# Attention loop: GpSimd forms the low weights of even slots, one maximum a slot, key projections every second slot

## The chip, the cores and the metric

The kernel runs on one core of one Trainium2 chip. The metric is the device time of one execution in microseconds (us). The engines are TensorE (PE, with its weight loads as PEld), VectorE (DVE), ScalarE (ACT), GpSimd (POOL) and SyncE (SP), which issues the transfers (DMA). Each runs its own instructions in order and waits on semaphores.

## The reference, cut to what matters

One layer in three parts, each added to x: a cross attention of 256 rows on 4096 context rows with 16 heads, a causal self attention, and routed experts. The change is in the first.

```python
kv_rope = kv_c * cos[None] + _rotate_half(kv_c) * sin[None]
q_r = jnp.einsum('bshq,hqr->bhsr', q_big, W_qr)
k_r = jnp.einsum('bld,hdr->bhlr', kv_rope, W_kr)
scores = jnp.einsum('bhsr,bhlr->bhsl', q_r, k_r)
attn = jax.nn.softmax(scores, axis=-1)
ctx_c = jnp.einsum('bhsl,bld->bhsd', attn, kv_rope)
```

## The kernel before, in words

Matmuls run in bf16, with each fp32 operand held as a high part and a low part (value minus high part). The heads are taken in 8 pairs. A pair is 16 slots; slots 0 to 7 are its first head, 8 to 15 its second, and a slot covers 512 context rows by 256 query rows.

For each slot, `scores` (PE, L944 and L945) writes one of two PSUM buffers `psS`; ACT takes the exponential twice, once as bf16 (`p_hi`, L491) and once as fp32 (`p_f`, L493); DVE forms `p_lo` = `p_f` minus `p_hi` (L687); `context_hi` (PE, L957 and L958) and `context_lo` (L965) add weights times values into the PSUM tile `psC`, a view of `psO[0]`. PE computes the scores of slot s + 1 at the start of slot s. After 8 slots the head's sums are copied out of `psC` (`head_out`, ACT, L484), a reciprocal is formed (DVE, L680) and GpSimd scales (`normalise`, L411). `context_hi` of the next head waits for that copy.

Beside this, the loop prepares the next pair. Its rotated keys come in 8 chunks of 512 rows: `keys` (PE, L903 to L905) writes the one bank `psO[1]`; ACT writes the high part `k_hi` (`keys_high`, L472); DVE writes the low part `k_lo` and so frees the bank (`keys_low`, L663, semaphore `s_kfree`). The softmax needs a bound on each row. For this, 16 `maximum` steps (two a chunk) each run two matmuls into `psM` (PE, L917) and one maximum over it (DVE, L669); `psM` is held once, so the next step's matmuls wait for the DVE. At the end DVE negates the maxima (L672, L674), PE turns them into a row (`bias`, L925), and ACT copies that row into row 64 of `q2` (`bias_rows`, L477), which the next pair's first `scores` waits for.

`keys` and `maximum` write shared `k_hi` and `k_lo`; the scores read copies of them. SP makes the copies in `copy_keys(q)` with DMAs from on-chip memory to on-chip memory: for each head j of the pair and each half of the chunks three transfers (L327 to L329), and for each head two more for its queries (L330, L331). SP issues them in this order and waits before each group of three:

```python
wait_apart(sp, s_kfree, q * CHUNKS + CHUNKS // 2 * (half + 1), sp_passed)
wait_apart(sp, s_scores, (q - 1) * SLOTS + HALF * j + HALF // 2 * (half + 1), sp_passed)
```

`keys_high` overwrites `k_hi`, so for the first chunk of a half it waits until both heads' copies of that half for the pair before are done:

```python
if c % (CHUNKS // 2) == 0:
    wait(act, k_copied[0][c // (CHUNKS // 2)], q * 48)
    wait(act, k_copied[1][c // (CHUNKS // 2)], q * 48)
```

The order of the work is written out by hand in the four `body` functions, one an engine. Before the change: chunk c is projected in slot c of the pair before, its `keys_high` and `keys_low` come one slot later, maxima 0 to 7 stand in slots 2 to 9 and two a slot in slots 10 to 13, the bias in slot 14. Pair 0 is written out, pairs 1 to 6 are a hardware loop, and pair 7, which prepares nothing, is written out.

Of the kernel before, what the change touches and what calls it, by code (L numbers as in the profile page):

```python
# [10 lines left out]
BF16 = mybir.dt.bfloat16  # L11
ACT = mybir.ActivationFunctionType
ALU = mybir.AluOpType
# [51 lines left out]
def maxima_in(slot):  # L65

    if 2 <= slot < 10:
        return [slot - 2]
    return [2 * slot - 12, 2 * slot - 11] if 10 <= slot < 14 else []


BIAS_SLOT = 14
# [50 lines left out]
def layer(nc, a, out):  # L123
    with ExitStack() as ctx:
# [13 lines left out]
        def cut(cols, at=None):  # L138
# [68 lines left out]
        raw = arena[:, top[0]:top[0] + TT * CW].rearrange("p (s w) -> p s w", s=TT)  # L207
        wo2 = cut(DC * D).rearrange("p (c n) -> p c n", c=DC)
# [52 lines left out]
        s_scores, s_phi, s_pf, s_plo, s_pv, s_out = (  # L261
            sem(n) for n in ("s_scores", "s_phi", "s_pf", "s_plo", "s_pv", "s_out"))
# [4 lines left out]
        qmax_copied = sem("qmax_copied")  # L267
# [110 lines left out]
        def _(pool):  # L378
# [12 lines left out]
            def bring(q):  # L391

                wait_apart(pool, s_mmm, q * MAXIMA, pool_passed)
                h = q * 2
                nc.gpsimd.tensor_copy(q_max, q1_all[:, bass.ds(h, 2), :]).then_inc(qmax_copied, 1)
                nc.gpsimd.tensor_copy(wkr_now[:, 0, :], wkr_hi[:, bass.ds(q * P, P)]).then_inc(qmax_copied, 1)
                nc.gpsimd.tensor_copy(wkr_now[:, 1, :], wkr_lo[:, bass.ds(q * P, P)]).then_inc(qmax_copied, 1)
            pool.wait_ge(qhi_done, 2)
# [15 lines left out]
            normalise(0)  # L414
            with pool.Fori(2, NPAIR) as q:
                bring(q)
                normalise(q * 2 - 3)
                normalise(q * 2 - 2)
            for h in range(H - 3, H):
                normalise(h)  # L420
# [11 lines left out]
        def _(act):  # L432
# [41 lines left out]
            def bias_rows(q):  # L474

                act.wait_ge(s_tmm, q + 1)
                nc.scalar.copy(q2[R:R + 1, :, :], psM[R:R + 1, :].rearrange("p (j s) -> p j s", j=2)[:, :, 0:T]).then_inc(s_bias, 1)  # L477

            def head_out(p, j):

                hd = p * 2 + j
                act.wait_ge(s_pv, hd * HALF + HALF)
                wait(act, ctx_done, hd)
                nc.scalar.copy(raw, psC).then_inc(s_out, 1)  # L484

            def body(p, ahead=True):
                for s in range(SLOTS):
                    t = p * SLOTS + s
                    act.wait_ge(s_scores, t + 1)
                    wait(act, s_pv, t - 1)  # L490
                    nc.scalar.activation(p_hi[:, s % 2, :], psS[s % 2][:, :], ACT.Exp).then_inc(s_phi, 1)  # L491
                    wait(act, s_plo, t - 1)
                    nc.scalar.activation(p_f[:, s % 2, :], psS[s % 2][:, :], ACT.Exp).then_inc(s_pf, 1)  # L493
                    if s == HALF:
                        head_out(p, 0)
                    if s == 0 and not (isinstance(p, int) and p == 0):
                        head_out(p - 1, 1)
                    if ahead and 1 <= s <= CHUNKS:
                        keys_high(p + 1, s - 1)
                    if ahead and s == BIAS_SLOT + 1:  # L500
                        bias_rows(p + 1)
            for what, n, *rest in BEFORE:
                if what == "rope":
                    rope_high(n)
                elif what == "k":
                    keys_high(0, n)
                elif what == "t":
                    bias_rows(0)
                elif what != "m" and (what != "hk" or rest[0] == DC - 1):
                    query(what, n)  # L510
            body(0)
            with act.Fori(1, NPAIR - 1) as p:
                body(p)
            body(NPAIR - 1, ahead=False)
            head_out(NPAIR - 1, 1)

# [78 lines left out]
        def _(dve):  # L595
# [80 lines left out]
            def one_over_sum(p, j):  # L676
                hd = p * 2 + j
                dve.wait_ge(s_out, hd + 1)
                wait(dve, ctx_done, hd)
                nc.vector.reciprocal(rsum, raw[:, :, K]).then_inc(s_rsum, 1)  # L680

            def body(p, ahead=True):
                for s in range(SLOTS):
                    t = p * SLOTS + s
                    dve.wait_ge(s_pf, t + 1)
                    wait(dve, s_pv, t - 1)
                    nc.vector.tensor_tensor(p_lo[:, s % 2, :], p_f[:, s % 2, :], p_hi[:, s % 2, :], ALU.subtract).then_inc(s_plo, 1)  # L687
                    if s == HALF:
                        one_over_sum(p, 0)
                    if s == 0 and not (isinstance(p, int) and p == 0):  # L690
                        one_over_sum(p - 1, 1)
                    if ahead and 1 <= s <= CHUNKS:
                        keys_low(p + 1, s - 1)
                    if ahead:
                        for m in maxima_in(s):
                            maximum(p + 1, m)
# [13 lines left out]
            body(0)  # L710
            with dve.Fori(1, NPAIR - 1) as p:
                body(p)
            body(NPAIR - 1, ahead=False)
            one_over_sum(NPAIR - 1, 1)
# [136 lines left out]
        def _(pe):  # L851
# [43 lines left out]
            def keys(q, c):  # L895

                first = isinstance(q, int) and q == 0
                bank = psE[c % 2] if first else psO[1]
                wait(pe, s_kfree, q * CHUNKS + c - (1 if first else 0))
                if c == 0:  # L900
                    pe.wait_ge(qmax_copied, q * 3 + 3)
                n = slice(512 * c, 512 * c + 512)
                mm(bank[:, :], wkr_now[:, 0, :], kt_hi[:, n], start=True, stop=False)  # L903
                mm(bank[:, :], wkr_now[:, 0, :], kt_lo[:, n], start=False, stop=False)
                mm(bank[:, :], wkr_now[:, 1, :], kt_hi[:, n], start=False, stop=True).then_inc(s_kmm, 1)  # L905

            def maximum(q, m):

                c, st = m // TT, m % TT
                wait(pe, s_mfree, q * MAXIMA + m)  # L910
                if m == 0:
                    wait(pe, s_bias, q)
                if st == 0:
                    pe.wait_ge(s_khi, q * CHUNKS + c + 1)
                for j in range(2):
                    r = slice(R * j, R * j + R)
                    last = mm(psM[:, 512 * j:512 * j + 512], q_max[r, j, P * st:P * st + P], k_hi[r, 512 * c:512 * c + 512], start=True, stop=True)  # L917
                last.then_inc(s_mmm, 1)

            def bias(q):  # L920

                pe.wait_ge(s_negm, q + 1)
                for j in range(2):
                    for st in range(TT):
                        last = mm(psM[R:R + 1, 512 * j + P * st:512 * j + P * st + P], negm[:, TT * j + st:TT * j + st + 1], ident_b, start=True, stop=True)  # L925
                last.then_inc(s_tmm, 1)
# [21 lines left out]
            def context_hi(p, s):  # L948
# [5 lines left out]
                for i in range(GROUP):  # L954
                    for st in range(TT):
                        ph = p_hi[:, s % 2, T * i + P * st:T * i + P * st + P]
                        mm(psC[:, st, :], ph, vx[:, GROUP * g + i, 0:CW], start=g == 0 and i == 0 and st == 0, stop=False, skip_group_check=True)  # L957
                        mm(psC[:, st, 0:K], ph, vx[:, GROUP * g + i, CW:VW], start=False, stop=False, skip_group_check=True)  # L958

            def context_lo(p, s):  # L960
                g, t = s % HALF, p * SLOTS + s
                pe.wait_ge(s_plo, t + 1)
# [6 lines left out]
            def body(p, ahead=True):  # L969
                for s in range(SLOTS):  # L970
                    now = maxima_in(s) if ahead else []
                    if s < SLOTS - 1:
                        scores(p, s + 1)
                    if now:
                        maximum(p + 1, now[0])
                    context_hi(p, s)
                    if s == SLOTS - 1 and ahead:
                        scores(p, SLOTS)
                    if ahead and s < CHUNKS:
                        keys(p + 1, s)  # L980
                    context_lo(p, s)
                    if now[1:]:
                        maximum(p + 1, now[1])
                    if ahead and s == BIAS_SLOT:
                        bias(p + 1)
            for what, n, *rest in BEFORE:
# [11 lines left out]
                elif what == "t":  # L998
                    bias(0)
                else:  # L1000
                    query(what, n, *rest)
# [3 lines left out]
            body(0)  # L1005
            with pe.Fori(1, NPAIR - 1) as p:
                body(p)
            body(NPAIR - 1, ahead=False)
# [286 lines left out]
```

## Time and profile before

| | us |
|---|---|
| median of three runs | 741.29 (740.64 to 742.59) |
| profiled execution | 741.01, its span 739.2 |
| PE, DVE, ACT, POOL busy | 654.4, 453.2, 384.5, 49.7 |
| mean granted TensorE clock | 0.979 of full speed; 1.00 in every stretch from 0 to 500 us |

The span runs from the first to the last instruction. Busy time counts overlaps once. The exponentials of the attention loop begin at 85.5 us and its last head is scaled at 502.2 us; the self attention and the experts follow.

### The profile page before, as it was taken

How to read it: one execution, taken by the hardware profiler on the slowest of the kernel's cores; microseconds unless marked ns; L12 is line 12 of the kernel's file. 1: busy time of each engine (PE TensorE's matmuls, PEld its weight loads, DVE VectorE, ACT ScalarE, POOL GpSimd, SP SyncE). 2: the span in 40 equal slices, each digit the busy share in tenths (PEclk: the TensorE clock that was granted, in tenths of full speed). 3: DMA queues.
4: the chain of work that ended last, by engine and by line, in shares of the span. 5: the costliest groups of instructions: out<-in, count | busy, mean ns of one | idle time of the engine just before them, and what ended most of it. 6: DMA issues, size and time to landing. Idle time of an engine off the chain costs nothing.

```text
span 739.2 us, 14931 instructions
## 1 busy us (share of the span) xinstructions
PE 654.4 (89%) x5890; PEld 461.1 (62%) x5890; DVE 453.2 (61%) x594; ACT 384.5 (52%) x567; POOL 49.7 (7%) x71
## 2 busy tenths in 40 slices
PE   5799899899898898898998998998978988899766
PEld 4666576676776776776776776885546856442211
DVE  2977598688688688698688687452127836211001
ACT  2543676676675675775775774882117842200000
POOL 2430000000000000000000000000002210000000
PEclk9999999999999999999999999999989989999989
DMA  8902794224224224233143143008980031299991
GB/s 360 418 26 43 172 336 99 49 45 91 49 43 90 48 46 87 48 64 79 38 82 79 24 93 80 7 2 327 416 348 4 1 115 57 104 395 419 415 418 68
DMA packets 25250, 105.04 MB, mean 142 GB/s; under 512 B 3712, under 2 KB 6912, under 8 KB 19200
## 3 DMA queue, kind: packets, MB, share of 16 engines
q1 hardware_dynamic: 25216, 104.57, 43.8%
q8 instruction: 24, 0.39, 0.2%
q14 instruction: 10, 0.08, 0.0%
HBM read 77.29 MB, written 0.52 MB: 105 GB/s over the span
## 4 chain that ended last, share of the span: by engine, by line
PE 59%; DVE 18%; issue 8%; ACT 7%; DMA 3%; SPq 3%; POOL 1%; DVEq 0%; ACTq 0%
PE psO L957 7%; PE psO L965 6%; DVE arena L669 6%; PE psO L958 5%; PE psS L945 5%; PE psS L944 5%; PE psM L917 5%; DVE arena L687 5%; PE psO L1029 4%; DMA arena<-w_exp 3%; SPq L351 3%; PE psS L1171 3%; PE psO L881 2%; PE psO L903 2%; PE psO L905 2%
## 5 line engine op out<-in xcount | busy, mean ns | idle before, releaser
L687 DVE TENSOR_TENSOR arena<-arena 128x1024 bf16<-128x1024 f32 x128 | 156.7, 1224 | 79.8 <-ACT arena L493 78.1
L491 ACT ACTIVATE arena<-psS 128x1024 bf16<-128x1024 f32 x128 | 131.2, 1025 | 113.2 <-PE psS L945 112.9
L669 DVE TENSOR_REDUCE arena<-psM 128x2 f32<-128x1024 f32 x128 | 155.9, 1218 | 14.8 <-PE psM L917 14.8
L957 PE MATMUL psO<-arena 128*128 128x129 bf16 x1024 | 133.4, 220 | 7.6 <-ACT arena L484 7.2
L958 PE MATMUL psO<-arena 128*128 128x128 bf16 x1024 | 132.5, 220 | 0.0
L493 ACT ACTIVATE arena<-psS 128x1024 f32<-128x1024 f32 x128 | 130.6, 1021 | 0.0
L944 PE MATMUL psS<-arena 128*128 128x256 bf16 x512 | 120.8, 273 | 0.8 <-ACT arena L477 0.8
L945 PE MATMUL psS<-arena 65*128 65x256 bf16 x512 | 120.8, 273 | 0.0
L957 PEld LDWEIGHTS psO<-arena 128*128 128x128 bf16 x1024 | 98.0, 98 | 30.3 <-issue 20.7
L958 PEld LDWEIGHTS psO<-arena 128*128 128x128 bf16 x1024 | 99.4, 97 | 0.4
L965 PE MATMUL psO<-arena 128*128 128x129 bf16 x1024 | 79.4, 220 | 8.8 <-DVE arena L687 8.4
L965 PEld LDWEIGHTS psO<-arena 128*128 128x128 bf16 x1024 | 65.2, 97 | 25.0 <-DVE arena L687 11.8
L917 PE MATMUL psM<-arena 64*128 64x512 bf16 x256 | 49.9, 386 | 16.2 <-DVE arena L669 15.8
L944 PEld LDWEIGHTS psS<-arena 128*128 128x128 bf16 x512 | 50.2, 98 | 12.4 <-issue 4.8
L945 PEld LDWEIGHTS psS<-arena 65*128 65x128 bf16 x512 | 50.1, 98 | 5.4
L917 PEld LDWEIGHTS psM<-arena 64*128 64x128 bf16 x256 | 12.3, 92 | 45.8 <-DVE arena L669 25.2
L1171 PE MATMUL psS<-arena 128*32 128x512 f32 x256 | 32.3, 649 | 8.4 <-DMA arena<-w_exp 7.9
L663 DVE TENSOR_TENSOR arena<-psO,arena 128x512 bf16<-128x512 f32 x56 | 38.2, 683 | 0.6
L567 ACT ACTIVATE arena<-psS 128x256 f32<-128x256 f32 x8 | 3.1, 383 | 64.2 <-PE psS L1171 64.2
L881 PE MATMUL psO<-arena 128*128 128x256 f32 x128 | 34.5, 400 | 0.7 <-ACT arena L440 0.7
L838 DVE TENSOR_TENSOR arena<-psS,arena 128x256 f32<-128x256 f32 x8 | 3.4, 424 | 51.4 <-ACT arena L567 51.4
L472 ACT CAST arena<-psO 128x512 bf16<-128x512 f32 x56 | 32.9, 588 | 3.1
(191 smaller groups left out, 767.9 us busy)
## 6 DMA issues: line engine op xcount, KB each, us to landing
arena<-w_exp SPq DMA_DIRECT2D x32, 1024.0 KB, 15.3
arena<-arena SPq DMA_DIRECT2D x96, 256.0 KB, 3.7
arena<-w_exp SPq DMA_DIRECT2D x32, 512.0 KB, 17.5
arena<-w_pair SPq DMA_DIRECT2D x8, 1088.0 KB, 16.8
arena<-w_o SPq DMA_DIRECT2D x1, 4096.0 KB, 21.1
arena<-w_shared SPq DMA_DIRECT2D x3, 1024.0 KB, 5.3
arena<-ctx SPq DMA_DIRECT2D x4, 512.0 KB, 13.5
arena<-rope SPq DMA_DIRECT2D x4, 512.0 KB, 14.3
```

The lines of the kernel that those rows point to most:

```text
L491: nc.scalar.activation(p_hi[:, s % 2, :], psS[s % 2][:, :], ACT.Exp).then_inc(s_phi, 1)
L493: nc.scalar.activation(p_f[:, s % 2, :], psS[s % 2][:, :], ACT.Exp).then_inc(s_pf, 1)
L669: nc.vector.reduce_max(maxes[:, :, st, c], psM[:, :].rearrange("p (j n) -> p j n", j=2), AX.X).then_inc(s_mfree, 1)
L687: nc.vector.tensor_tensor(p_lo[:, s % 2, :], p_f[:, s % 2, :], p_hi[:, s % 2, :], ALU.subtract).then_inc(s_plo, 1)
L881: last = mm(psO[h % 2][:, 0:T], wq[:, c, K * j:K * j + K], xnT[:, c, :], start=c == 0, stop=c == DC - 1)
L917: last = mm(psM[:, 512 * j:512 * j + 512], q_max[r, j, P * st:P * st + P], k_hi[r, 512 * c:512 * c + 512], start=True, stop=True)
L944: mm(o, k1[:, j, l], q1[:, j, :], start=True, stop=False)
L945: last = mm(o, k2[0:R + 1, j, l], q2[0:R + 1, j, :], start=False, stop=True)
L957: mm(psC[:, st, :], ph, vx[:, GROUP * g + i, 0:CW], start=g == 0 and i == 0 and st == 0, stop=False, skip_group_check=True)
L958: mm(psC[:, st, 0:K], ph, vx[:, GROUP * g + i, CW:VW], start=False, stop=False, skip_group_check=True)
L965: last = mm(psC[:, st, :], p_lo[:, s % 2, T * i + P * st:T * i + P * st + P], vx[:, GROUP * g + i, 0:CW], start=False, stop=g == HALF - 1 ...
L1171: last = mm(psF[g % 2][SLOT * j:SLOT * j + SLOT, :], xpT[:, c, CAP * e:CAP * e + SLOT], ring[e % RING][:, 2 * FI * c:2 * FI * (c + 1)], st ...
```

## The change

A table made by `plan` now says for each slot which chunks and which maxima of the next pair (1) and of the pair after that (2) stand in it. In the steady loop chunk c of the next pair stands in slot 2c - 4 for c from 2 to 7, maximum m from 2 to 15 in slot m - 2, and the first two chunks of the pair after next in slots 12 and 13, its first two maxima in slots 14 and 15. `keys_high` and `keys_low` now stand in the slot of their `keys`. GpSimd forms `p_lo` of the even slots, DVE that of the odd ones. `context_lo` of an even slot comes at the end of the next slot, that of an odd slot in the next slot behind `scores`. DVE takes `head_out` and `bias_rows` over from ACT, and the bias row is written to `psO[1]`. The exponential into `p_hi` waits for `context_hi` (`s_hi`) instead of `context_lo`. GpSimd brings a second set of queries and key weights for the early chunks. `copy_keys` and the waits in `keys_high` stay. Pairs 1 to 5 are the loop; pairs 0, 6 and 7 are written out.

```diff
+def plan(first, after):
+    keys = [(1, c, c if first else 2 * c - 4) for c in range(0 if first else 2, CHUNKS)]
+    keys += [(2, c, SLOTS - 4 + c) for c in range(2)] if after else []
+    at = [2, 3, 4, 4, 5, 6, 6, 7, 8, 8, 9, 10, 10, 11, 12, 13] if first else [None, None, *range(BIAS_SLOT)]
+    maxima = [(1, m, slot) for m, slot in enumerate(at) if slot is not None]
+    maxima += [(2, m, BIAS_SLOT + m) for m in range(2)] if after else []
+ENTRY, STEADY, LAST_BUT_ONE, LAST = plan(True, True), plan(False, True), plan(False, False), [[[], []]] * SLOTS
...
+            def low_part(p, s):
+                wait_apart(pool, s_pf, p * SLOTS + s + 1, pool_passed)
+                wait_apart(pool, s_pv, p * SLOTS + s - 1, pool_passed)
+                nc.gpsimd.tensor_tensor(p_lo[:, s % 2, :], p_f[:, s % 2, :], p_hi[:, s % 2, :], ALU.subtract).then_inc(s_plo[0], 1)
+            def body(p, after=True):
+                for s in range(0, SLOTS, 2):
+                    if s == 0 and not (isinstance(p, int) and p == 0):
+                        normalise(p * 2 - 1)
+                    if s == HALF:
+                        normalise(p * 2)
+                    low_part(p, s)
+                    if after and s == 4:
+                        bring_next(p + 2)
+                    if after and s == BIAS_SLOT - 2:
+                        bring(p + 2)
...
 (ACT, in body)
-                    wait(act, s_pv, t - 1)
+                    wait(act, s_hi, t - 1)
+                    wait(act, s_plo[s % 2], p * HALF + s // 2)
-                    wait(act, s_plo, t - 1)
-                    if ahead and 1 <= s <= CHUNKS:
-                        keys_high(p + 1, s - 1)
+                    for d, c in todo[s][0]:
+                        keys_high(p + d, c)
...
 (DVE, in body; head_out comes first in slots 0 and 8)
+                    if s == BIAS_SLOT and todo is not LAST:
+                        bias_rows(p + 1)
+                    for d, m in maxima[0:1]:
+                        maximum(p + d, m)
+                    if s % 2:
+                        dve.wait_ge(s_pf, t + 1)
+                        wait(dve, s_pv, t - 1)
+                        nc.vector.tensor_tensor(p_lo[:, s % 2, :], p_f[:, s % 2, :], p_hi[:, s % 2, :], ALU.subtract).then_inc(s_plo[1], 1)
+                    for d, c in keys:
+                        keys_low(p + d, c)
+                    for d, m in maxima[1:2]:
+                        maximum(p + d, m)
...
 (PE, in body)
+                    key_steps, maxima = todo[s]
                     if s < SLOTS - 1:
                         scores(p, s + 1)
+                    elif todo is not LAST:
+                        scores(p, SLOTS)
+                    if s % 2 == 0 and s:
+                        context_lo(p, s - 1)
+                    if s == 0 and not (isinstance(p, int) and p == 0):
+                        context_lo(p - 1, SLOTS - 1)
+                    if s == BIAS_SLOT and todo is not LAST:
+                        bias(p + 1, todo is not LAST_BUT_ONE)
+                    for d, m in maxima[0:1]:
+                        maximum(p + d, m)
+                    for d, c in key_steps:
+                        keys(p + d, c)
                     context_hi(p, s)
+                    for d, m in maxima[1:2]:
+                        maximum(p + d, m)
+                    if s % 2:
+                        context_lo(p, s - 1)
```

The order of ACT in the loop, slots 7 to 10 before: L491 and L493 are the exponentials, L484 is `head_out`, L472 is `keys_high`, whose first waits of the pair stand in slot 1.

```order
L491 ACTIVATE arena<-psS 128x1024 [waits s_pv,s_scores]
L493 ACTIVATE arena<-psS 128x1024 [waits s_plo]
L482 ISA
L484 COPY arena<-psO 128x258 [waits ctx_done,s_pv]
L467 REGISTER_ALU
L472 CAST arena<-psO 128x512 [waits s_kmm]
L489 REGISTER_ALU
L491 ACTIVATE arena<-psS 128x1024 [waits s_pv,s_scores]
L493 ACTIVATE arena<-psS 128x1024 [waits s_plo]
L489 REGISTER_ALU
L491 ACTIVATE arena<-psS 128x1024 [waits s_pv,s_scores]
```

Slots 12 and 13 of ACT after the change, where the first two chunks of the pair after next stand (L511 and L512 are the exponentials, L503 is `keys_high`):

```order
L511 ACTIVATE arena<-psS 128x1024 [waits s_plo_even]
L512 ACTIVATE arena<-psS 128x1024
L498 ISA
L114 REGISTER_ALU [waits s_kmm]
L503 CAST arena<-psO 128x512 [waits k_copied10,k_copied00]
L508 REGISTER_ALU
L511 ACTIVATE arena<-psS 128x1024 [waits s_plo_odd,s_hi,s_scores]
L512 ACTIVATE arena<-psS 128x1024
L498 REGISTER_ALU
L503 CAST arena<-psO 128x512 [waits s_kmm]
```

The copy out of `psC` is gone from ACT, and the first chunk's `keys_high`, with its wait for the copies of both heads, stands in front of the exponentials of slot 13.

The order of DVE in the loop, slots 9 to 11 before: L687 is `p_lo`, L669 the maximum.

```order
L687 TENSOR_TENSOR arena<-arena 128x1024 [waits s_pv,s_pf]
L668 REGISTER_ALU
L669 TENSOR_REDUCE arena<-psM 128x2 [waits s_mmm]
L685 REGISTER_ALU
L687 TENSOR_TENSOR arena<-arena 128x1024 [waits s_pv,s_pf]
L668 REGISTER_ALU
L669 TENSOR_REDUCE arena<-psM 128x2 [waits s_mmm]
L668 REGISTER_ALU
L669 TENSOR_REDUCE arena<-psM 128x2 [waits s_mmm]
L685 REGISTER_ALU
L687 TENSOR_TENSOR arena<-arena 128x1024 [waits s_pv,s_pf]
```

Slots 3 to 5 of DVE after (L680 is the maximum, L717 `p_lo` of an odd slot, L674 `keys_low`):

```order
L680 TENSOR_REDUCE arena<-psM 128x2 [waits s_mmm]
L715 REGISTER_ALU
L717 TENSOR_TENSOR arena<-arena 128x1024 [waits s_pv,s_pf]
L679 REGISTER_ALU
L680 TENSOR_REDUCE arena<-psM 128x2 [waits s_mmm]
L672 REGISTER_ALU
L674 TENSOR_TENSOR arena<-psO,arena 128x512 [waits s_khi]
L679 REGISTER_ALU
L680 TENSOR_REDUCE arena<-psM 128x2 [waits s_mmm]
L715 REGISTER_ALU
L717 TENSOR_TENSOR arena<-arena 128x1024 [waits s_pv,s_pf]
```

There is one maximum in each slot, it stands ahead of `p_lo`, and only every second slot has a `p_lo` on this engine.

## Rows read from the trace of the kernel before

**Rows 1.** The page: busy time, share, instructions.
```profile
PE 654.4 (89%) x5890; PEld 461.1 (62%) x5890; DVE 453.2 (61%) x594; ACT 384.5 (52%) x567; POOL 49.7 (7%) x71
```

**Rows 2.** Waits of PE, 187 to 241 us: engine, line, waited for, us, times, longest.
```profile
PE psM L917 <- DVE arena L669: 2.1, 6, 0.4
PE psO L965 <- DVE arena L687: 1.0, 1, 1.0
PE psO L957 <- ACT arena L484: 1.0, 1, 1.0
```

**Rows 3.** Timeline of POOL: start, us, engine, line, op [idle before].
```profile
196.24 0.61 POOL L411 TENSOR_TENSOR arena<-arena 128x256 f32 x1 [8.24 <-DVE arena L680]
...
250.05 0.61 POOL L411 TENSOR_TENSOR arena<-arena 128x256 f32 x1 [8.24 <-DVE arena L680]
```

**Rows 4.** Timeline of PE in a slot with keys and one maximum, in order.
```profile
206.52 0.27 PE L944 MATMUL psS<-arena 128*128 128x256 bf16 x1
...
207.51 0.39 PE L917 MATMUL psM<-arena 64*128 64x512 bf16 x2
207.83 0.23 PE L957 MATMUL psO<-arena 128*128 128x129 bf16 x1
...
208.77 0.38 PE L903 MATMUL psO<-arena 128*128 128x512 bf16 x1
...
209.42 0.62 PE L965 MATMUL psO<-arena 128*128 128x129 bf16 x8
209.87 0.27 PE L944 MATMUL psS<-arena 128*128 128x256 bf16 x1
```

**Rows 5.** Timeline of PE in slot 14.
```profile
189.61 0.63 PE L965 MATMUL psO<-arena 128*128 128x129 bf16 x8 [1.04 <-DVE arena L687]
190.17 0.38 PE L925 MATMUL psM<-arena 128*1 128x128 bf16 x4
```

**Rows 6.** Timeline of DVE, slots 13 and 14.
```profile
183.84 1.22 DVE L687 TENSOR_TENSOR arena<-arena 128x1024 bf16<-128x1024 f32 x1
184.97 1.22 DVE L669 TENSOR_REDUCE arena<-psM 128x2 f32<-128x1024 f32 x1
186.68 1.23 DVE L669 TENSOR_REDUCE arena<-psM 128x2 f32<-128x1024 f32 x1 [0.49 <-PE psM L917]
```

**Rows 7.** Timeline of ACT: two slots with two maxima, then slot 8.
```profile
179.71 1.02 ACT L491 ACTIVATE arena<-psS 128x1024 bf16<-128x1024 f32 x1 [2.04 <-PE psS L945]
...
183.69 1.02 ACT L491 ACTIVATE arena<-psS 128x1024 bf16<-128x1024 f32 x1 [2.04 <-PE psS L945]
...
220.40 0.59 ACT L472 CAST arena<-psO 128x512 bf16<-128x512 f32 x1
```

**Rows 8.** Timeline of DVE, the low part of chunk 7.
```profile
221.02 0.69 DVE L663 TENSOR_TENSOR arena<-psO,arena 128x512 bf16<-128x512 f32 x1
```

**Rows 9.** Timeline of SP's transfer issues from there.
```profile
221.95 0.50 SPq L327 DMA_DIRECT2D arena<-arena  x1
...
227.90 0.61 SPq L329 DMA_DIRECT2D arena<-arena  x1
```

**Rows 10.** Line L329, 221 to 230 us: landing after issue.
```profile
DMA to landing us min/median/max: 4.3/4.4/4.6
```

**Rows 11.** Stretches: PE, PEld, DVE, ACT, POOL busy, PEclk, DMA share, GB/s.
```profile
231.00:232.00 1.00, 0.72 (x13) 0.54 (x10) 1.00 (x1) 0.49 (x1) 0.00 (x0) 1.00 0.61 127
```

**Rows 12.** Timeline of POOL and of DVE ahead of the loop.
```profile
14.17 2.27 POOL L387 TENSOR_TENSOR arena<-arena 128x512 f32<-128x512 f32 x2 [13.73 <-DMA arena<-rope]
16.70 3.56 POOL L387 TENSOR_TENSOR arena<-arena 128x512 f32<-128x512 f32 x2 [0.27 <-DMA arena<-rope]
...
19.27 2.06 DVE L644 TENSOR_TENSOR arena<-arena 128x1024 f32<-128x1024 f32 x1
```

**Rows 13.** Timeline of DVE in the last pair.
```profile
473.23 1.23 DVE L687 TENSOR_TENSOR arena<-arena 128x1024 bf16<-128x1024 f32 x1 [1.31 <-ACT arena L493]
...
478.04 1.23 DVE L687 TENSOR_TENSOR arena<-arena 128x1024 bf16<-128x1024 f32 x1 [1.31 <-ACT arena L493]
```

More of the change, by code:

```diff
@@ L62 @@
 MAXIMA = CHUNKS * TT
[L65 to L72, printed above, removed]
+def plan(first, after):
[4 more added lines that the diff above has]
+    maxima += [(2, m, BIAS_SLOT + m) for m in range(2)] if after else []
+    return [[[(d, n) for d, n, slot in what if slot == s] for what in (keys, maxima)] for s in range(SLOTS)]
+BIAS_SLOT = SLOTS - 2
+ENTRY, STEADY, LAST_BUT_ONE, LAST = plan(True, True), plan(False, True), plan(False, False), [[[], []]] * SLOTS
 def before_loop():
@@ L413, in _ @@
             bring(1)
[L414 to L420, printed above, removed]
+            def body(p, after=True):
[9 more added lines that the diff above has]
+                        bring(p + 2)
+            body(0)
+            with pool.Fori(1, NPAIR - 2) as p:
+                body(p)
+            body(NPAIR - 2, after=False)
+            body(NPAIR - 1, after=False)
+            normalise(H - 1)
             for h in range(NH2):
@@ L472, in keys_high, with body @@
                 nc.scalar.copy(k_hi[:, 512 * c:512 * c + 512], bank[:, :]).then_inc(s_khi, 1)
[L474 to L486, printed above, removed]
+            def body(p, todo):
                 for s in range(SLOTS):
@@ L506, in _ @@
                     keys_high(0, n)
-                elif what == "t":
-                    bias_rows(0)
-                elif what != "m" and (what != "hk" or rest[0] == DC - 1):
+                elif what not in "mt" and (what != "hk" or rest[0] == DC - 1):
                     query(what, n)
[L511 to L515, printed above, removed]
+            body(0, ENTRY)
+            with act.Fori(1, NPAIR - 2) as p:
+                body(p, STEADY)
+            body(NPAIR - 2, LAST_BUT_ONE)
+            body(NPAIR - 1, LAST)
             for h in range(H):
@@ L674, in maximum, with bias_rows, head_out @@
                     nc.vector.tensor_scalar_mul(negm, mx4, -1.0).then_inc(s_negm, 1)
-            def one_over_sum(p, j):
+            def bias_rows(q):
+                wait(dve, s_scores, q * SLOTS)
+                dve.wait_ge(s_tmm, q + 1)
+                nc.vector.tensor_copy(q2[R:R + 1, :, :], psO[1][R:R + 1, :].rearrange("p (j s) -> p j s", j=2)).then_inc(s_bias, 1)
+            def head_out(p, j):
                 hd = p * 2 + j
+                dve.wait_ge(s_pv, hd * HALF + HALF)
+                wait(dve, ctx_done, hd)
+                nc.vector.tensor_copy(raw, psC).then_inc(s_out, 1)
@@ L678, in one_over_sum, with body @@
                 dve.wait_ge(s_out, hd + 1)
-                wait(dve, ctx_done, hd)
                 nc.vector.reciprocal(rsum, raw[:, :, K]).then_inc(s_rsum, 1)
-            def body(p, ahead=True):
+            def body(p, todo):
                 for s in range(SLOTS):
                     t = p * SLOTS + s
-                    dve.wait_ge(s_pf, t + 1)
-                    wait(dve, s_pv, t - 1)
-                    nc.vector.tensor_tensor(p_lo[:, s % 2, :], p_f[:, s % 2, :], p_hi[:, s % 2, :], ALU.subtract).then_inc(s_plo, 1)
+                    if s == 0 and not (isinstance(p, int) and p == 0):
+                        head_out(p - 1, 1)
@@ L688, in body @@
                     if s == HALF:
[L689 to L696, printed above, removed]
+                        head_out(p, 0)
+                    keys, maxima = todo[s]
@@ L709, in _ @@
                     maximum(0, n)
[L710 to L714, printed above, removed]
+                elif what == "t":
+                    bias_rows(0)
+            body(0, ENTRY)
+            with dve.Fori(1, NPAIR - 2) as p:
+                body(p, STEADY)
+            body(NPAIR - 2, LAST_BUT_ONE)
+            body(NPAIR - 1, LAST)
+            head_out(NPAIR - 1, 1)
             for h in range(H):
@@ L957, in context_hi @@
                         mm(psC[:, st, :], ph, vx[:, GROUP * g + i, 0:CW], start=g == 0 and i == 0 and st == 0, stop=False, skip_group_check=True)
-                        mm(psC[:, st, 0:K], ph, vx[:, GROUP * g + i, CW:VW], start=False, stop=False, skip_group_check=True)
+                        last = mm(psC[:, st, 0:K], ph, vx[:, GROUP * g + i, CW:VW], start=False, stop=False, skip_group_check=True)
+                last.then_inc(s_hi, 1)
             def context_lo(p, s):
-                g, t = s % HALF, p * SLOTS + s
-                pe.wait_ge(s_plo, t + 1)
+                g = s % HALF
+                pe.wait_ge(s_plo[s % 2], p * HALF + s // 2 + 1)
                 for i in range(GROUP):
@@ L967, in context_lo, with body @@
                 last.then_inc(s_pv, 1)
-            def body(p, ahead=True):
+            def body(p, todo):
                 for s in range(SLOTS):
-                    now = maxima_in(s) if ahead else []
+                    key_steps, maxima = todo[s]
                     if s < SLOTS - 1:
                         scores(p, s + 1)
-                    if now:
-                        maximum(p + 1, now[0])
-                    context_hi(p, s)
[L977 to L985, printed above, removed]
+                    elif todo is not LAST:
+                        scores(p, SLOTS)
+                    if s % 2 == 0 and s:
+                        context_lo(p, s - 1)
+                    if s == 0 and not (isinstance(p, int) and p == 0):
+                        context_lo(p - 1, SLOTS - 1)
[5 more added lines that the diff above has]
+                        keys(p + d, c)
+                    context_hi(p, s)
+                    for d, m in maxima[1:2]:
+                        maximum(p + d, m)
+                    if s % 2:
+                        context_lo(p, s - 1)
             for what, n, *rest in BEFORE:
@@ L1004, in _ @@
             scores(0, 0)
[L1005 to L1008, printed above, removed]
+            body(0, ENTRY)
+            with pe.Fori(1, NPAIR - 2) as p:
+                body(p, STEADY)
+            body(NPAIR - 2, LAST_BUT_ONE)
+            body(NPAIR - 1, LAST)
+            context_lo(NPAIR - 1, SLOTS - 1)
             pe.wait_ge(ctx_done, H)
```

55 lines of the change are left out of this document (34 added, 21 removed).

## Prediction

> **What bounds the kernel now.** I read the page's busy times first, then who waited for whom on PE in one steady pair, then the timelines of the engines in single slots, and last SP's transfers. The page has PE busy for 89% of the span and DVE for 61% [rows 1]. A steady pair lasts 250.05 - 196.24 = 53.81 us, from one head's scaling on GpSimd to the same one a pair later [rows 3], and PE's named waits in it sum to 4.1 us: six for `psM`, one for the low weights in slot 14, one for the copy out of `psC` [rows 2].
>
> PE's own work in a pair comes from one slot that has everything [rows 4]. Scores and one maximum take 207.83 - 206.52 = 1.31 us; 0.32 of it follows the maximum's recorded start, and with about 0.1 in front (nearest: an L965 group is 0.1 longer behind a wait, below) I give the maximum 0.42 and the scores 0.89. `context_hi` takes 0.94, the keys 0.65, `context_lo` 0.45. The bias takes about 0.3 [rows 5]. A pair is 16 x (1.31 + 0.94 + 0.45) + 8 x 0.65 + 0.3 = 48.7 us. The other 5.1 us are waiting: a slot with two maxima takes 183.69 - 179.71 = 3.98 us [rows 7] where its work is 3.35 - 0.65 + 0.42 = 3.12, so 0.86, three times; 1.04 in slot 14 [rows 5]; 1.0 for the copy [rows 2]; the rest is restarting. So PE is the bound in most slots, and the most that this change can give is about 5 us a pair.
>
> **The change part by part.** Durations come from one execution of 741.01 us, its span 739.2 with 1.8 around it; the median of the runs is 0.3 higher. I sum against 741.01.
>
> *Removed in a steady pair.* With one maximum a slot the DVE has a whole slot for it, `context_lo` of slot 14 has a slot to spare, and the copy out of `psC` on DVE lies beside a maximum and keys (1.07 us). All 5.1 us go. Moving `head_out` and `bias_rows` from ACT to DVE puts about 1 us a head on an engine that gives up 8 x 1.13 us of low weights, so I cost it at nothing. The wait on `s_hi` in place of `s_pv` only relaxes ACT.
>
> *Added first: `context_lo` of odd slots.* On DVE the maximum of an odd slot now stands ahead of `p_lo`. From the end of PE's matmuls for it, PE has `context_hi`, `context_lo` and scores to do: 0.94 + 0.45 + 0.89 = 2.28 us. The DVE path is 0.11 to its start (it starts 0.49 behind the previous one's end, where 0.06 passes to PE and 0.32 are the matmuls), 1.13 to the next start, 1.22 for `p_lo` [rows 6] and 0.06 back: 2.52. PE waits 0.24 us and then reloads: the group L965 takes 0.56 us behind a wait [rows 5] against 0.45 [rows 4]. That is 0.35 us at each of 8 places. Bounds: 0 (if PE is late anyway) and 0.6.
>
> *Added second: the early chunks wait for the key copies.* This is the term that decides. `keys_high` of chunk 0 of the pair after next overwrites `k_hi`, so it waits for both heads' copies of the next pair. The second head's first group of copies stands in SP's queue behind the first head's second group, and that one waits for `s_kfree` of chunk 7, which now falls in slot 10 and no longer in slot 8. Chunk 0 stands only two slots behind it. In the trace the same queue runs like this: DVE ends chunk 7 at 221.71 us [rows 8], SP issues the first copy at 221.95, two queries' transfers follow, the last needed copy is issued at 227.90 [rows 9] and lands 4.4 us later [rows 10]: 10.6 us from DVE's end. Before the change `keys_high` of the next chunk 0 stood nine slots behind chunk 7, over 25 us.
>
> From PE's start of chunk 7 to its start of chunk 1, which needs the bank that DVE frees for chunk 0: keys 0.65, to ACT 0.2, `keys_high` 0.59 [rows 7] with 0.03, `keys_low` 0.69 [rows 8], copies 10.6, `keys_high` and `keys_low` again 1.4, restart 0.1: 14.2 us. PE's work in between is three `context_hi` (2.82), three scores (2.67), three maxima (1.26), two chunks (1.30), two `context_lo` (0.90), 8.95. Meanwhile ACT, in order, holds the exponentials of slot 13 behind that same wait, and DVE the maximum and `p_lo` of slot 13; both are short enough to follow.
>
> *The steady pair* is then 14.2, plus the rest of PE's work 48.7 - 8.95 = 39.75, plus six odd waits that lie outside (2.1; slot 11's is swallowed, slot 13's is met): 56.05 us against 53.81, +2.2. Five such pairs: +11.2.
>
> *Entry (pair 0).* Two more chunks and two more maxima on PE, 1.30 + 0.84 = 2.14. Four of its slots hold two maxima and about seven times the matmuls wait some 0.4 for the DVE (0.86 less the second maximum's work, [rows 6]); with three odd waits and the head copy that is 4.0 of waiting against 5.1. I take +1.0; its early chunks meet the copies later, since its chunk 7 is done in slot 8.
>
> *Pair 6* has two chunks and two maxima fewer (they were done early) and no early ones: 48.7 - 2.1 = 46.6, with eight odd waits 49.4. That is -4.4.
>
> *Last pair.* Two slots take 478.04 - 473.23 = 4.81 us [rows 13], PE's work in them 4.56. At most 16 x 0.12 = 1.9 can go; GpSimd's slower `p_lo` stands against it at both head ends. I take 0.
>
> *GpSimd's low weights.* No 128 x 1024 subtraction on GpSimd is in the trace. Undisturbed, two products of 128 x 512 took 2.27 us, beside DVE additions two took 3.56 [rows 12]. So one of 1024 takes 2.27 or 3.56 us. I take 2.3: in the steady pair it starts when `p_f` of an even slot is there and DVE's next `p_lo` comes one slot, 3 us, later. PE needs it two slots on. The tight place is behind a head's end, where GpSimd first scales: copy, reciprocal, passing it on (put at 0.3) and 0.61 of scaling [rows 3] end about 0.7 us behind PE's restart, the weights are there at 3.0, and PE asks at 0.94 + 0.89 + 0.42 + 0.94 = 3.2. With 2.3 it costs 0, with 2.7 about 0.2 to 0.4 twice a pair.
>
> Sum: 11.2 + 1.0 - 4.4 + 0 = +7.8, so 748.8 on the profiled run and 749 against the median.
>
> **The rivals.** *The copies are in time (faster).* If the 10.6 us of copies were 5 us shorter, or ACT did not need them, a steady pair would be 48.7 + 8 x 0.35 = 51.5: five times -2.3, with entry and pair 6 -14.9, 726. It decides at 5.7 us of copies, since PE has 8.95 + 0.35 of its own there and 3.6 of the chain is computation. For it: the issue of the six transfers and two queries' is over after some 6.6 us, and only bytes are left. Against it: the transfers still move at 127 GB/s in the stretch from 231 to 232 us [rows 11], ten us behind the first issue, so it is bytes and not a late signal.
>
> The Trainium skill ("SBUF — State Buffer", section "SBUF: two separate sides") gives the DMA side about 436 GB/s in one direction. By that rate the same 1.6 MB would take 3.8 us, not 8.2, and the result would be near this rival's. The trace shows 201 GB/s at full occupancy for such copies, which read and write on the chip.
>
> *The odd wait isn't there.* If PE gets to `context_lo` of an odd slot later than I reckon, six waits a pair and eight in pair 6 go: 749 - 10.5 - 2.8 = 736. For it: my 0.24 is the difference of two sums of 2.3 and 2.5. Against it: each piece is a row.
>
> *GpSimd and DVE disturb each other (slower still).* The row with 3.56 overlaps a DVE addition that took 2.06 us in place of 1.2 [rows 12]. If each `p_lo` on GpSimd takes 3.56, PE waits 1.1 us more behind each of 14 head ends, 15 us; in the last pair the ring of GpSimd (3.56), both exponentials (1.9) and signals (0.3) takes 5.8 us for two slots in place of 4.8, +8: 749 + 23 = 772. Against it: the overlap in a steady pair is at most 0.2 us, in three places. It decides where `p_lo` on GpSimd takes over 2.5 us.
>
> The skill's same page, section "Who interferes with whom", says that a DVE instruction with two SBUF inputs contends with a GpSimd instruction that reads SBUF, and the one that comes second stands still until the first is through. Rows 12 agree in kind. By it, what matters is whether they meet, and by my walk they meet fully only in the last pair, behind its two head ends, for about 1 us in all.
>
> **How the numbers follow.** The forecast 0.55, its own range 743 to 757 (odd waits halved: -6; GpSimd at 2.8: +8). Copies in time 0.12 at 726, no odd wait 0.13 at 736, GpSimd and DVE 0.13 at 772, and 0.07 for something that brings it back to about 741. Two in ten left out: the range is 735 to 760. This kernel's measurement can tell 0.3%, 2.2 us, from no change. Slower: 0.55 + 0.13 + 0.02 = 0.70. Same: 0.07. Faster: 0.12 + 0.11 = 0.23.
>
> **What would show it.** In the profile after: a steady period near 56 us; in each of the five loop pairs ACT idle for 5 us or more ahead of one `keys_high` in slot 12, released by a transfer, and PE idle about 5 us ahead of a keys matmul; the six waits for `psM` gone in those pairs; waits of about 0.2 us of L1005 for DVE; GpSimd's subtraction at 2.2 to 2.5 us. A steady period under 53 with no such gap proves the forecast wrong, and so does a subtraction of 3 us or more.

## The result and the profile after

The changed kernel takes 759.09 us (757.6 to 760.55, four runs) against 741.07 us before in the same session: 1.0228 times, 95% interval 1.0207 to 1.0249. I forecast slower, 749. The direction holds, and the time lies inside the range of 735 to 760, but the slowdown of 18.0 us is more than twice the 7.8 that I summed. The profiled execution took 760.55, its span 758.7.

First the page of the changed kernel, busy time by engine, which answers to [rows 1].

```profile
PE 673.9 (89%) x5890; PEld 472.1 (62%) x5890; DVE 398.7 (53%) x554; ACT 368.4 (49%) x543; POOL 192.2 (25%) x153
```

DVE gave up 54 us and GpSimd took 142, as the edit says. PE has the same 5890 matmuls and yet is busy 19.5 us longer. That equals the growth of the span only because PE's idle time is 84.8 us in both kernels: new idle time stands where the removed waits were. PE's work did not grow, so part of it ran slower.

The five periods of the loop, read as in [rows 3] but from the scaling of one first head to the next, are 56.75, 57.36, 57.67, 57.87 and 57.71 us, before 53.82. Where one of them waits, by engine (waits of PE from 225 to 258 us, of ACT from 257 to 315 us; engine, line, waited for, us in total, times, longest), answers to [rows 2]:

```profile
PE psO L941 <- DVE arena L674: 4.8, 1, 4.8
```
```profile
ACT arena L503 <- PE psO L943: 12.5, 7, 2.4
ACT arena L503 <- DMA arena<-arena: 7.6, 1, 7.6
```

PE's old named waits are gone from the loop and one of 4.8 us has come, in each of the five pairs. Here is how it comes about, in the timelines of the changed kernel: DVE ends chunk 7, SP issues eight transfers, ACT takes chunk 0 of the pair after next, DVE frees the bank. They answer to [rows 8, 9].

```profile
289.80 0.69 DVE L674 TENSOR_TENSOR arena<-psO,arena 128x512 bf16<-128x512 f32 x1
...
301.65 0.69 DVE L674 TENSOR_TENSOR arena<-psO,arena 128x512 bf16<-128x512 f32 x1 [5.69 <-ACT arena L503]
```
```profile
290.73 0.50 SPq L334 DMA_DIRECT2D arena<-arena  x1
...
296.65 0.61 SPq L336 DMA_DIRECT2D arena<-arena  x1
```
```profile
301.04 0.58 ACT L503 CAST arena<-psO 128x512 bf16<-128x512 f32 x1 [7.59 <-DMA arena<-arena]
301.52 1.03 ACT L511 ACTIVATE arena<-psS 128x1024 bf16<-128x1024 f32 x1
```

From DVE's end at 290.49 to ACT's start are 10.55 us (forecast 10.6). ACT's next exponential stands behind it, as the order showed. What the forecast did not have is in the stretches of the pair before this one (us, then busy time and instructions of PE, PEld, DVE, ACT, POOL, the granted clock, DMA share, GB/s):

```profile
242.00:243.00 1.00, 0.00 (x0) 0.00 (x0) 0.00 (x0) 0.00 (x0) 0.00 (x0) 0.71 1.00 209
243.00:244.00 1.00, 0.00 (x0) 0.00 (x0) 0.00 (x0) 0.30 (x1) 0.00 (x0) 0.50 0.02 4
...
245.00:246.00 1.00, 0.94 (x3) 0.39 (x4) 1.00 (x2) 1.00 (x2) 0.00 (x0) 0.50 0.00 0
...
248.00:249.00 1.00, 1.00 (x12) 1.00 (x10) 0.39 (x1) 0.99 (x2) 0.00 (x0) 0.50 0.00 0
249.00:250.00 1.00, 1.00 (x11) 0.83 (x9) 0.00 (x0) 0.00 (x0) 0.70 (x1) 0.87 0.00 0
```

PE stood idle from 240.2 to 245.06 us. While it did, the granted clock fell from 2.4 to 1.2 GHz, and it stayed there for 4.2 us of full work, until 249.3 us. The matmuls show it too (timeline of PE, to be held against 0.38 and 0.22 in [rows 4]):

```profile
245.47 0.63 PE L942 MATMUL psO<-arena 128*128 128x512 bf16 x1
...
246.32 0.32 PE L996 MATMUL psO<-arena 128*128 128x129 bf16 x1
```

The span's growth of 19.5 us by parts: up to the first head's end of pair 1, +1.2 (forecast +1.0); five loop periods 287.4 against 269.1, +18.3 (+11.2); the next, -4.9 (-4.4); the last pair +0.1 (0); the part behind the loop 241.8 against 237.0, +4.8 (0). Two terms are off: the loop period, and the part behind. The +1.2 agrees with its forecast by chance, as the section on why the prediction was wrong shows.

### The profile page after: what moved, and what is told of

It is laid out like the page before. It is cut to its first block, busy times and chain, and to the rows that moved or that the text cites. A ratio compares the mean times of both kernels' runs of the same rounds, so it can differ in the third digit from the quotient of the medians.

```text
span 758.7 us, 14924 instructions
## 1 busy us (share of the span) xinstructions
PE 673.9 (89%) x5890; PEld 472.1 (62%) x5890; DVE 398.7 (53%) x554; ACT 368.4 (49%) x543; POOL 192.2 (25%) x153
## 4 chain that ended last, share of the span: by engine, by line
PE 56%; DVE 17%; issue 8%; SPq 6%; DMA 6%; ACT 5%; POOL 1%; DVEq 0%; ACTq 0%
DVE arena L717 7%; PE psO L1005 6%; PE psM L954 5%; PE psO L996 5%; PE psO L997 4%; PE psS L983 4%; PE psS L984 4%; PE psO L1076 4%; DMA arena<-arena 3%; SPq L358 3%; DMA arena<-w_exp 3%; PE psS L1218 3%; DVE arena L680 3%; PE psO L909 2%; PE psO L941 2%
## 5 line engine op out<-in xcount | busy, mean ns | idle before, releaser
L680 DVE TENSOR_REDUCE arena<-psM 128x2 f32<-128x1024 f32 x128 | 156.6, 1223 | 75.9 <-PE psM L954 75.8
L417 POOL TENSOR_TENSOR arena<-arena 128x1024 bf16<-128x1024 f32 x64 | 138.4, 2162 | 172.5 <-ACT arena L512 137.2
L511 ACT ACTIVATE arena<-psS 128x1024 bf16<-128x1024 f32 x128 | 132.0, 1032 | 32.1 <-PE psS L984 20.1
L996 PE MATMUL psO<-arena 128*128 128x129 bf16 x1024 | 136.7, 224 | 1.5 <-ACT arena L511 1.2
L997 PE MATMUL psO<-arena 128*128 128x128 bf16 x1024 | 136.2, 224 | 0.0
L512 ACT ACTIVATE arena<-psS 128x1024 f32<-128x1024 f32 x128 | 132.3, 1034 | 0.0
L983 PE MATMUL psS<-arena 128*128 128x256 bf16 x512 | 122.5, 276 | 1.4 <-DVE arena L691 1.4
L984 PE MATMUL psS<-arena 65*128 65x256 bf16 x512 | 122.4, 275 | 0.0
L996 PEld LDWEIGHTS psO<-arena 128*128 128x128 bf16 x1024 | 101.2, 100 | 21.7 <-issue 15.2
L997 PEld LDWEIGHTS psO<-arena 128*128 128x128 bf16 x1024 | 101.5, 99 | 7.5 <-issue 1.4
L717 DVE TENSOR_TENSOR arena<-arena 128x1024 bf16<-128x1024 f32 x64 | 82.2, 1284 | 20.7 <-ACT arena L512 20.7
L503 ACT CAST arena<-psO 128x512 bf16<-128x512 f32 x56 | 32.8, 586 | 123.7 <-PE psO L943 85.8
L1005 PE MATMUL psO<-arena 128*128 128x129 bf16 x1024 | 81.7, 224 | 4.4 <-DVE arena L717 1.0
L1005 PEld LDWEIGHTS psO<-arena 128*128 128x128 bf16 x1024 | 64.0, 99 | 18.2 <-DVE arena L717 17.2
L674 DVE TENSOR_TENSOR arena<-psO,arena 128x512 bf16<-128x512 f32 x56 | 38.5, 688 | 36.8 <-ACT arena L503 33.5
L984 PEld LDWEIGHTS psS<-arena 65*128 65x128 bf16 x512 | 50.6, 99 | 5.8
L941 PE MATMUL psO<-arena 128*128 128x512 bf16 x56 | 22.9, 409 | 24.1 <-DVE arena L674 24.1
L909 PE MATMUL psO<-arena 128*128 128x256 f32 x128 | 36.1, 415 | 0.7 <-ACT arena L471 0.7
## 6 DMA issues: line engine op xcount, KB each, us to landing
arena<-w_exp SPq DMA_DIRECT2D x32, 512.0 KB, 17.1
arena<-rope SPq DMA_DIRECT2D x4, 512.0 KB, 14.1
```

Of the source, the lines that this page charges most:

```text
L417: nc.gpsimd.tensor_tensor(p_lo[:, s % 2, :], p_f[:, s % 2, :], p_hi[:, s % 2, :], ALU.subtract).then_inc(s_plo[0], 1)
L680: nc.vector.reduce_max(maxes[:, :, st, c], psM[:, :].rearrange("p (j n) -> p j n", j=2), AX.X).then_inc(s_mfree, 1)
L983: mm(o, k1[:, j, l], q1[:, j, :], start=True, stop=False)
L984: last = mm(o, k2[0:R + 1, j, l], q2[0:R + 1, j, :], start=False, stop=True)
L997: last = mm(psC[:, st, 0:K], ph, vx[:, GROUP * g + i, CW:VW], start=False, stop=False, skip_group_check=True)
L1005: last = mm(psC[:, st, :], p_lo[:, s % 2, T * i + P * st:T * i + P * st + P], vx[:, GROUP * g + i, 0:CW], start=False, stop=g == HALF - 1 ...
```

## The experiments

Theory 1: PE waits for the key copies, and its clock falls in that idle time. Theory 2: the loss lies with GpSimd's share of the low weights. A second profile of the changed kernel, unaltered, asks whether the longer part behind the loop was chance.

**Copies first.**

```diff
-                for j in range(2):
-                    for half in range(2):
+                for j, half in ((0, 0), (1, 0), (0, 1), (1, 1)):
...
```

The waits in front of each group stay, and the queries' transfers still follow each head's second group.

> The changed kernel with one edit: SP issues the second head's first group of key copies ahead of the first head's second group, under the same waits. Theory 1 (the early chunks wait for that group, and PE's clock falls in the idle time): the group can start when the scores of slot 11 are done, lands ahead of slot 12's keys, ACT's wait of 7.6 us and PE's of 4.8 us go, the clock stays at full speed in the loop, a steady pair takes 51.5 to 52 us in place of 56.8 to 57.9, the kernel 727 to 733. Theory 2 (the loss lies in GpSimd's share of the low weights, and the copies only stand where something else would): steady pair 56 or more, over 750.

Measured: 721.04 us (720.14 to 722.96), 0.972 of before, 0.9699 to 0.9741. The loop periods are 50.6 us. From 200 to 251 us ACT's waits name no transfer any more, and PE ran through at full clock (stretch of this kernel, columns as above):

```profile
197.00:248.00 51.00, 49.35 (x571) 37.74 (x577) 36.47 (x40) 34.77 (x41) 20.26 (x16) 1.00 0.31 66
```

So the order in which SP issues its copies is worth 38 us, with everything else of the change in place; 34.4 of it lies in the five loop periods. Theory 2 falls as the explanation of the loss. It came out 6 us below what I expected, 0.9 us a pair.

**Idle matmuls in the gap (80).**

```diff
                     for d, c in key_steps:
+                        if not isinstance(p, int) and d == 2 and c == 1:
+                            for _ in range(80):
+                                mm(psO[0][:, 384:512], ident_b, ident_b, start=False, stop=False, skip_group_check=True)
                         keys(p + d, c)
```

> The changed kernel with 80 idle matmuls of 128 columns (some 4.6 us at full clock, into columns of the bank that nothing reads) ahead of the keys matmuls of the second early chunk in the five loop pairs, where PE stands idle 4.8 us for the copies. The result's values are untouched, the work is added. Theory 1: the time of the copies stays, but the granted clock stays at 1.00, so a steady pair takes 56.0 us, as worked out without the clock, in place of 56.8 to 57.9, and the kernel 750 to 754. Theory 2 (the low clock costs nothing, since the rest waits anyway): 759, or more by what the matmuls delay.

Measured: 745.14 us (743.92 to 746.02), 1.0044 of before, 1.0027 to 1.0061. A wait of ACT from 225 to 281 us in this kernel, and a stretch of 32 us with one gap in it:

```profile
ACT arena L503 <- DMA arena<-arena: 7.6, 1, 7.6
```
```profile
225.35:257.52 32.17, 30.97 (x389) 24.84 (x391) 19.64 (x23) 18.99 (x23) 11.89 (x9) 1.00 0.39 80
```

The copies are waited for as long as before, 7.6 us, and added work made the kernel 14.0 us faster, to 5 us below what I expected. Its loop periods are 57.0 (pair 1, where ACT waits 9.2 us for the copies), then 55.4 three times and 55.2. So at full clock a pair with the wait is 1.6 us longer than before (and 4.8 longer than with copies first), and in pairs 2 to 5 the low clock adds 2.0, 2.3, 2.5 and 2.5. That fits the changed kernel's stretches: in those pairs PE works at the low clock for 4.2, 4.9, 5.2 and 5.4 us behind the gap, and half of that would be 2.1 to 2.7. Pair 1 doesn't show it, since its wait differs in the two kernels. Of the 14.8 us between the two profiles only 9.0 lie in the loop, where the added matmuls are; 1.2 lie ahead of it and 4.6 behind it.

**Idle matmuls, half as many (40).**

> As the kernel with 80 idle matmuls, with 40: PE works 2.3 us more and then stands idle some 2.5 us in each of the five loop pairs, about as long as at the end of the last pair in every kernel. If only the length of the gap sets the price, the clock falls for a shorter stretch or not at all, a steady pair takes 55.4 to 56.5 us and the kernel 745 to 752. If any gap of that kind drops the clock as the whole one does, a steady pair takes 57.4 to 57.9 and the kernel 757 to 760. Rival to both (the clock has nothing to do with it, the 14 us of the other kernel came from elsewhere): no lower clock in the loop, yet 757 or more.

Measured: 750.99 us (749.79 to 754.01), 1.0116 of before, 1.0092 to 1.0141. PE's gap is now 4.3 us in pair 1 and 2.7 to 2.8 in the others. The loop periods are 58.6, 55.37, 57.04, 55.37 and 56.82. The stretches behind the five gaps in this kernel:

```profile
189.00:194.00 5.00, 4.55 (x39) 4.08 (x41) 3.49 (x6) 3.65 (x6) 1.11 (x1) 0.66 0.00 0
246.00:251.00 5.00, 4.57 (x60) 3.89 (x62) 4.25 (x8) 5.00 (x7) 1.14 (x1) 1.00 0.11 25
302.00:306.00 4.00, 4.00 (x33) 3.44 (x32) 2.88 (x5) 3.01 (x4) 0.71 (x1) 0.58 0.00 0
359.00:364.00 5.00, 5.00 (x67) 4.24 (x66) 4.25 (x7) 4.82 (x6) 1.73 (x1) 1.00 0.23 48
415.00:419.00 4.00, 4.00 (x37) 3.50 (x34) 2.26 (x5) 2.70 (x5) 1.34 (x1) 0.57 0.00 0
```

The clock fell in three and stayed in two. The kernel's time lies in the range of my first reading (the length of the gap sets the price), but two periods, 57.04 and 56.82, lie between the two readings. A gap of 2.7 to 2.8 us dropped the clock in two of four pairs. Where it did, the low clock lasted 3.4 us, and the pair was 1.6 to 1.7 us longer than the same pair with 80 idle matmuls. The one gap of 4.3 us (pair 1) dropped it too.

**No early chunks.** Pairs 0 to 6 all use the entry's table without its part for the pair after next; `bring_next` and the waits on it are left out.

```diff
-ENTRY, STEADY, LAST_BUT_ONE, LAST = plan(True, True), plan(False, True), plan(False, False), [[[], []]] * SLOTS
+ENTRY, STEADY, LAST_BUT_ONE, LAST = plan(True, False), plan(True, False), plan(True, False), [[[], []]] * SLOTS
```

> The changed kernel without the early chunks: each of pairs 0 to 6 prepares its next pair by the entry's table (chunk c in slot c, two maxima in slots 4, 6, 8 and 10); GpSimd, head_out and bias_rows as in the change. Theory 1: no wait for copies, no idle gap, clock at 1.00; PE's work of 48.7 us and some 4 us of waits give a steady pair of 52 to 53, pair 6 is longer by 3 than in the change, and the kernel takes 733 to 740. Theory 2 (loss in GpSimd's share): over 750.

Measured: 734.08 us (734.01 to 734.9), 0.9904 of before, 0.9885 to 0.9923; loop periods 52.78. As expected (733 to 740). Without the early chunks the rest of the change is faster than before, though two maxima share a slot again.

**Copies first, and the odd low weights ahead of the maximum.**

```diff
-                    for d, m in maxima[0:1]:
-                        maximum(p + d, m)
                     if s % 2:
                         ...
+                    for d, m in maxima[0:1]:
+                        maximum(p + d, m)
```

> As the kernel with the copies reordered, and DVE forms the low weights of an odd slot ahead of that slot's maximum. If the wait of PE for odd low weights is 0.24 us and 0.1 of reload at eight places a pair, a steady pair takes 49 to 49.8 us and the kernel 714 to 722. Rival: the maximum, now later, makes PE wait for psM instead, and it takes as long as the kernel with the copies reordered alone.

Measured: 716.32 us (714.6 to 717.21), 0.9656 of before, 0.9633 to 0.968: the fastest of all. The time is as expected, but only since the kernel with copies first was faster than expected too: the loop periods, 50.05, are only 0.6 less than without the swap, where eight waits of 0.35 make 2.8. The wait is real: in the changed kernel PE's weight loads L1005 wait 2.5 us in seven places for L717 (from 200 to 255 us), 0.36 each, and in PE's timeline such a group starts 0.24 us late and takes 0.56. The swap takes these waits away, but not their price: an odd group now takes 0.63 us in place of 0.24 + 0.56, which gives back 0.17 and not 0.35, and PE waits 0.6 us for `keys_low` ahead of the bias (L965 for L675), which it did not without the swap. Why the group takes 0.63 and not 0.45 stays open.

**The same with GpSimd's share taken back.**

```diff
-                    if s % 2:
-                        ...  .then_inc(s_plo[1], 1)
+                    ...  .then_inc(s_plo[s % 2], 1)
...
-                    low_part(p, s)
...
+                if m == 2 and not (isinstance(q, int) and q < 2):
+                    pe.wait_ge(qmax_copied, q * 3 + 3)
```

The last two lines add a wait of PE for GpSimd's copies of the queries ahead of the third maximum; from 200 to 255 us PE's waits name no GpSimd line.

> The kernel with copies reordered and the odd low weights ahead of the maximum, with GpSimd's share taken back: DVE forms the low weights of all slots, ahead of the slot's maximum. DVE then has 16 x 1.14 + 16 x 1.14 + 8 x 0.6 and about 2 us more, 43 us in a pair of 50. Theory 1 (order and copies made the gain, GpSimd only relieves): a steady pair 50 to 51.5, the kernel 716 to 726. Rival (GpSimd's share carries the gain): a steady pair over 53, 740 or more.

Measured: 727.69 us (726.95 to 728.44), 0.9801 of before, 0.9782 to 0.9822; loop periods 51.54. A little over my bound of 726. DVE is busy 43.85 us in 51 where it was busy 36.47 in the kernel with copies first (a stretch of this kernel):

```profile
201.00:252.00 51.00, 47.66 (x559) 37.57 (x564) 43.85 (x47) 33.66 (x41) 5.96 (x8) 1.00 0.31 66
```

GpSimd's share is worth 11.4 us beside the kernel with the swap, 1.5 us a loop pair and 3.2 in the entry: a gain, and no cause of loss.

**Before, with copies first.**

> The kernel before with the same reordering of SP's copies. Nothing waits for them there, so 741, within 0.3%. If the reordering itself were worth something, or cost something at the heads' starts, it would show here.

Measured: 741.44 us, 0.9998 of before, 0.9985 to 1.0011; loop periods 53.82. The order matters only where something waits for it.

**The changed kernel again.**

> The changed kernel once more, unaltered, for a second profile. The part behind the attention loop took 241.8 us in the first profile against 237.0 before, with the same instructions. If that is chance in the granted clock, it will be nearer to 237 to 240 now while the steady pairs stay at 56.7 to 57.9; if the change does something to that part, it will be 241 to 242 again.

Measured once: 760.41 us; loop periods 57.38 to 57.93, and 241.9 us behind the loop. So that was not chance. In both profiles the clock is at half from 519 to 522 us, right behind the loop; with 80 idle matmuls the same stretch behind the last head (507 to 516 us) has 1.00, and the part takes 237.2. The instructions there are the same. Over all profiles the part was longer where the clock fell right behind the loop, 241.8, 241.9, 240.2 (40 idle matmuls) and 239.4 us (copies first), than where it didn't, 237.0 to 237.2, and 238.1 and 238.2 in the kernels with the swap. But that one fall is not all of it: the clock also falls further on, in every kernel. What the granted clock lacks of full speed, summed over the part by single microseconds, is 15.3 us in the four profiles with 237.0 to 237.2, 17.1 and 18.8 in those with 238.1 and 238.2, 18.8 in those with 239.4 and 240.2, and 19.2 and 20.9 in the two of the changed kernel. So the part is longer where more of it ran at the low clock. Why the clock falls there more often in some kernels than in others stays open, and so does whether the gaps in the loop have to do with it (it fell behind the loop with copies first too, which has none); I made no run that tells.

## Why the prediction was wrong, step by step

*What bounds the kernel* was right: PE, with waits that the change removes. In the loop all its named waits but the new one are gone.

*The copies*, the deciding term, was right in place and size: 10.55 us where 10.6 were summed. In the profile after, PE starts chunk 7 at 230.97 and chunk 1 at 245.06: 14.1 us, where 14.2 were summed.

*The step that failed* is "The steady pair is then 14.2, plus the rest of PE's work 48.7 - 8.95 = 39.75, plus six odd waits": a steady pair at +2.2 us. It measured +3.7 on the mean (18.3 by five). I had put a gap of 5 us into PE's row and then charged the work behind it at the rate of [rows 4], which is the rate of an engine that never stood still. The kernel with 80 idle matmuls shows the sum without that: 55.4, +1.6, so the rest of PE's work was even 0.6 too dear; the low clock adds 2.0 to 2.5 in pairs 2 to 5. The missing rival was not another wait but a price on the wait that I had found.

*"The part behind the loop"* stood in the sum at 0 with no word. It measured +4.8, and +4.9 in the second profile. In the one profile with 80 idle matmuls 4.6 of it are gone; that the filling did it is not shown.

*Odd low weights*: 0.24 + 0.11 forecast, 0.24 + 0.11 measured in PE's timeline. As a thing to be gained by a swap it was oversized more than fourfold (2.8 us a pair against 0.6).

*Pair 6, last pair*: -4.9 and +0.1 against -4.4 and 0. Right. *Entry*: +1.2 against +1.0 is luck. In the profile after, the granted clock was 0.87 and 0.79 of full speed from 20 to 30 and from 30 to 40 us, ahead of the attention loop, and the first exponential starts at 87.22 us against 85.47 before. From there to the scaling of pair 0's second head it is 56.20 us against 56.97, so the entry itself gave 0.8 where it was to cost 1.0; the second profile, whose clock did not fall there, has 56.19.

*GpSimd's subtraction* was put at 2.3 and takes 2.13 us in 61 of its 64 places; the other three take 2.75, 2.75 and 3.08. The last of them is over the 3 us that the prediction named as a sign of being wrong. The contention that I drew from [rows 12] comes where I put it, behind the head ends of the last pair, where it falls on DVE, and also in the entry and in pair 6, where it falls on GpSimd (the last pair of the changed kernel, GpSimd and DVE, then its pair 6, DVE and GpSimd):

```profile
480.26 2.13 POOL L417 TENSOR_TENSOR arena<-arena 128x1024 bf16<-128x1024 f32 x1
```
```profile
480.50 2.97 DVE L717 TENSOR_TENSOR arena<-arena 128x1024 bf16<-128x1024 f32 x1 [0.88 <-ACT arena L512]
```
```profile
472.00 1.22 DVE L717 TENSOR_TENSOR arena<-arena 128x1024 bf16<-128x1024 f32 x1
```
```profile
472.12 3.08 POOL L417 TENSOR_TENSOR arena<-arena 128x1024 bf16<-128x1024 f32 x1 [3.00 <-ACT arena L512]
```

In the last pair DVE starts 0.24 us behind GpSimd, shares 1.89 us with it and takes 1.75 longer than its 1.22. In pair 6 GpSimd starts 0.12 behind DVE, shares 1.10 us with it and takes 0.95 longer than its 2.13. So the one that started second lost nearly the whole overlap, and the first lost nothing. The Trainium skill ("SBUF — State Buffer", section "Who interferes with whom") has this as a rule: the second one stands still until the first is through. The trace agrees with it in both orders. In the last pair it costs next to nothing: 18.04 us for a head, before 17.95.

*The rival "copies in time"* at 726 is what the edit on SP made real: 721.0. The rate of 436 GB/s that the prediction holds against the measured 201 had no part in the sum. Each key copy spans only 64 of the 128 partitions, which the prediction did not weigh; no run here varies it.

## What to carry to other kernels

When a schedule is pulled forward, look for the overwrite that it pulls forward too: here the data's readers were early enough, but the copy that had to be done before the overwrite stood in another engine's queue behind copies of the other half. And when a sum puts a gap of some microseconds into TensorE's row, the gap has two prices, its length (here 4.8 us) and the slow matmuls behind it (here 2.0 to 2.5 us). Filling it with idle matmuls tells them apart in one run, and reordering the queue that causes it removed both. A second profile of the same kernel is worth its run: it showed that the entry's +1.2 was chance and the part behind the loop was not.

## What the runs showed of the hardware that I had not expected

Work that nobody needs made a kernel 14.0 us faster; 9.0 us of the difference between the profiles lie in the loop, where it kept the clock at 2.4 GHz. In the changed kernel's two profiles a gap of 4.8 us dropped it each time, ten in all. With 40 idle matmuls one of 4.3 us did, and those of 2.7 to 2.8 us did in two of four, in the same program with the same instructions ahead of them; with 80, one of 2.1 us did not. The low clock, once there, lasted for 2.9 to 5.5 us of full work behind a gap of 4.8 us, and for 3.4 us behind the shorter ones.
